# Extra products for TensorE in the last body and the tail of a cross-attention and mixture-of-experts kernel

## The reference

```python
def block(x, ctx):
    h = layernorm(x)
    q = rms_norm(h @ q_w.T + q_b, norm_q_w)
    k_img, v_img = rms_norm(ctx[:, :257] @ k_img_w.T + k_img_b, norm_k_img_w), ctx[:, :257] @ v_img_w.T + v_img_b
    k, v = rms_norm(ctx[:, 257:] @ k_w.T + k_b, norm_k_w), ctx[:, 257:] @ v_w.T + v_b
    x = x + (attention(q, k_img, v_img) + attention(q, k, v)) @ o_w.T + o_b
    h = layernorm(x)
    gate = top2(softmax(h @ Wg + bg))            # 8 experts
    for e in range(8):
        y = gelu(h @ W1[e] + b1[e]); y = gelu(y @ W2[e] + b2[e]); y = y @ W3[e] + b3[e]
        x = x + gate[:, e] * y
    return x
```

## Time and profile before

| | before |
|---|---|
| median of 3 runs | 842.35 us (840.61 to 843.66) |
| time of the profiled execution | 840.39 us |
| its span, first to last instruction | 838.5 us |
| PE busy | 759.5 us, 91% of the span |
| DVE, ACT, POOL busy | 599.0, 491.5, 240.5 us |
| mean granted clock of PE | 0.958 of full speed |

### The profile page before, as it was taken

One profiled execution on the slowest core, in us unless ns is written; L12 is line 12 of the kernel. 1 busy time (PEld: TensorE's weight loads), 2 busy tenths in 40 slices (PEclk: granted clock), 3 DMA queues, 4 the chain that ended last, 5 costly groups with the idle time before them and its releaser, 6 DMA issues.

```text
span 838.5 us, 17282 instructions
## 1 busy us (share of the span) xinstructions
PE 759.5 (91%) x5906; PEld 658.8 (79%) x5906; DVE 599.0 (71%) x1269; ACT 491.5 (59%) x1136; POOL 240.5 (29%) x302
## 2 busy tenths in 40 slices
PE   4889899989898989775499999999999999999994
PEld 3657677767676767454499999999999999999993
DVE  6767878787878796765576868576676858676664
ACT  4377777777777767585154645555554555554443
POOL 3523334343434242214300504032140505032010
PEclk9989999999999999776599999999999999999998
DMA  9720102011111110232755665748575665748561
GB/s 315 281 81 6 58 4 68 27 51 44 35 61 35 60 32 17 87 121 84 258 194 189 246 223 222 247 154 291 212 249 198 245 230 217 253 163 288 197 218 64
DMA packets 29205, 126.28 MB, mean 151 GB/s; under 512 B 4204, under 2 KB 4220, under 8 KB 19424
## 3 DMA queue, kind: packets, MB, share of 16 engines
q1 hardware_dynamic: 23696, 109.80, 37.1%
q0 software_dynamic: 5456, 15.81, 5.3%
HBM read 108.42 MB, written 18.74 MB: 152 GB/s over the span
## 4 chain that ended last, share of the span: by engine, by line
PE 70%; DVE 11%; ACT 10%; issue 5%; DMA 2%; POOL 1%; SPq 0%; ACTq 0%; DVEq 0%; POOLq 0%
PE tiles L1174 7%; PE tiles L1176 6%; PE tiles L1175 6%; PE scores L1463 4%; PE scores L1461 4%; PE ptb L1289 4%; PE scores L1462 4%; PE pvb L1176 3%; PE pvb L1175 3%; PE ptb L1175 3%; PE pvb L1174 3%; PE ptb L1174 3%; PE ptb L1176 3%; PE scores L1279 2%; PE pvb L1312 2%
## 5 line engine op out<-in xcount | busy, mean ns | idle before, releaser
L918 DVE TENSOR_TENSOR w<-scr,w 128x2048 fp32r<-128x2048 f32 x75 | 170.8, 2289 | 59.4 <-ACT w L682 59.4
L682 ACT ACTIVATE w<-scr 128x2048 fp32r<-128x2048 f32 x76 | 144.8, 1908 | 54.9 <-PE scores L1463 54.9
L512 POOL DMA_INDIRECT out_dram<-scr,tok x17 | 18.0, 1059 | 301.7 <-DVE scr L1153 299.3
L664 ACT ACTIVATE scr<-scr,rsum 112x257 f32<-112x257 f32 x128 | 66.4, 519 | 61.7 <-DVE rsum L902 61.7
L1174 PE MATMUL tiles<-c,w 128*128 128x258 f32 (+2 forms) x272 | 80.4, 296 | 4.7 <-DVE c L1127 2.6
L1174 PE MATMUL tiles<-w 128*128 128x256 f32 (+1 forms) x288 | 82.9, 288 | 0.6
L1175 PE MATMUL tiles<-w 128*128 128x256 f32 (+1 forms) x288 | 81.2, 282 | 0.0
L1176 PE MATMUL tiles<-w 128*128 128x256 f32 (+1 forms) x288 | 81.2, 282 | 0.0
L1141 DVE CAST w<-scr 128x256 fp32r<-128x256 f32 (+1 forms) x144 | 42.0, 292 | 54.6 <-ACT scr L772 54.6
L1289 PE MATMUL ptb<-ident,scr 112*128 112x112 f32 x384 | 63.9, 277 | 18.0 <-ACT scr L672 16.4
L1175 PE MATMUL tiles<-c,w 128*128 128x258 f32 (+2 forms) x272 | 77.8, 286 | 0.0
(11 more groups left out here) (221 smaller groups left out, 2302.2 us busy)
## 6 DMA issues: line engine op xcount, KB each, us to landing
scr<-in_dram SPq DMA_DIRECT2D x76, 1024.0 KB, 4.9
scr<-in_dram SPq DMA_DIRECT2D x8, 750.0 KB, 5.1
scr<-slots_d SPq DMA_DIRECT2D x10, 528.0 KB, 5.4
scr<-in_dram SPq DMA_DIRECT2D x10, 512.0 KB, 8.2
slots_d<-rows SPq DMA_DIRECT2D x8, 528.0 KB, 11.6
xn<-in_dram SPq DMA_DIRECT2D x9, 256.0 KB
xb<-in_dram SPq DMA_DIRECT2D x8, 224.0 KB, 2.7
xr<-in_dram SPq DMA_DIRECT2D x8, 224.0 KB, 2.6
```

Of the source, the lines that this page charges most:

```text
L664: act.activation(probs[0:L, s, 0:IMG], probs[0:L, s, 0:IMG], ACT.Copy, scale=rsum[0:L, g, s, 0:1]).then_inc(S["normal_img"], 1)
L682: act.activation(EH[slot], raw[slot], ACT.Copy).then_inc(S["eh_done"], 1)
L918: dve.tensor_tensor(EL[slot], raw[slot], EH[slot].bitcast(F32), ALU.subtract).then_inc(S["el_done"], 1)
```

## The change

PE gets 89 extra products. Each multiplies 128 columns with 512 columns of `wH(WV)`, weights that lie in SBUF and that nothing overwrites until the first expert's activations are written; the result goes into that one of the two `tiles` banks that has nothing pending, and nothing reads it. Their places are the ends of slots, after the fill: two in each slot 1 to 15 of body LAST (30 products, bank 1), then 2, 2, 4, 11, 2 and 8 in slots 0, 1, 2, 6, 12 and 15 of body DONE (29, bank 0), 24 between the count of tokens and the wait for `slots_done`, and 6 behind the first `turn`. Two waits guard the banks: one for the copy of the last values out of bank 1 (ACT L639), ahead of the first pair, and one for `take_o` of sequence 6, at the start of DONE's. No other engine's stream changes.

```diff
+BUSY_AT = {LAST: {h: 2 for h in range(1, 16)}, DONE: {0: 2, 1: 2, 2: 4, 6: 11, 12: 2, 15: 8}}
...
+            def keep_busy(bank, n):
+
+                spare = wH(WV)
+                for _ in range(n):
+                    pe.matmul(tiles[:, bank, :], spare[:, 0:P], spare[:, 0:512], start=True, stop=True)
...
                     for name, lo, hi in FILL[h]:
                         if has(name, b) and not (fixed(b, DONE) and hi < NC):
                             stage(name, lo, hi, b, p)
+                    if fixed(b, LAST) and h == 1:
+                        bank, cnt = tile_use("o", DONE)
+                        pe.wait_ge(tile_free[bank], cnt)
+                    if fixed(b, DONE) and h == 0:
+                        taken(pe, "o", LAST)
+                    if b in BUSY_AT and h in BUSY_AT[b]:
+                        keep_busy(tile_use("o", DONE if fixed(b, LAST) else LAST)[0], BUSY_AT[b][h])
...
             pe.matmul(ptb[:, 0:E], ones[0:L, :], sofar[0:L, :], start=True, stop=True).then_inc(S["count_ready"], 1)
...
+            keep_busy(tile_use("o", LAST)[0], 24)
             pe.wait_ge(S["slots_done"], 1)
...
             turn(0, BLOCK)
+            keep_busy(tile_use("o", LAST)[0], 6)
```

## The result

The change takes 836.93 us in the median of 11 runs (834.62 to 839.66), the kernel before 841.6 us beside it (840.37 to 843.66). The ratio is 0.9948, 95% interval 0.9935 to 0.9961: faster by 0.5%, or 4.4 us by the ratio (4.7 between the medians). The forecast was -2.8 us, with a range of 835.2 to 844.0.

A forecast was written before the change was run, and what follows sets the result against it. PE was taken to bound most of the kernel, neither full nor fast at about 335 to 419 us. LAST +0.5 and the tail -3.3 gave -2.8 us, a median of 839.5 us, range 835.2 to 844.0.

The forecast's parts named there:

- The tail: After sequence 7's take_o: full clock shortens turn by 1.1 us and the experts' first 24 products by 2.3; -3.3 us with risk.
- What the change can give in LAST: Body LAST to DONE slot 0: terms +0.86, +1.0, +0.35 and -1.4 sum to +0.8 us, taken as +0.5.
- The fall at 348.0: LAST slots 0 and 1: one pair is too little, clock still falls; slots 2 to 4 stay at half, costing 0.86 us.
- Slots 10 to 12: Body LAST: even odds that the clock holds, gaining 2.0 less 1.0 us, or falls, losing 1.7; mean +0.35.
- The price of a pair: Six on-path pairs in LAST and DONE slot 0: 0.5 us each at full clock, 3.0 in all; 5.2 at half.
- the forecast's list: PE work on the path at half clock in LAST and DONE slot 0; full clock would save 7.0 us together.
- the best case of -4.0: Body LAST with the clock at full: 7.0 us gained less 3.0 for the six on-path pairs.
- Between the last output product and the turn: 387 to 406 us: DVE and POOL set the end, so fast clock gives nothing and products fitting the gaps are free.
- Risk of the 24: Products ahead of the first turn: half at half clock they take 8.0 of 7.97 us; 0 to 0.7 late, 0.1 charged.
- the first rival: Clock holds nearly throughout LAST: -4.0 - 3.3 = -7.3 us, so 835.0; chance 0.20.
- The rival in which the pairs are paid at half: LAST slots 3 to 11 and DONE 0: clock not held, 5.2 us paid, total +2.5, so 844.9; chance 0.15.
- The tail's gain: Rival that it is missing: half clock at turn or the 24 late; tail 0, LAST +0.5, 842.9; chance 0.15.

The follow-up runs named there:

- tail_only: The change without the 30 extra products of body LAST: 838.91 us against 842.0 before, ratio 0.9964.
- change_again: The change itself, unaltered, timed again beside the kernel before: 838.07 us against 840.84, ratio 0.9954.
- last_only: The change with only the 30 products of body LAST, none in DONE or around the first turn: 840.33 us against 842.0 before, ratio 0.9989.
- twelve: The change with 12 instead of 24 products ahead of the first turn: 838.65 us against 842.98 before, ratio 0.9951.
- no_small: The change without the 11, 2 and 8 products in slots 6, 12 and 15 of DONE: 837.63 us against 842.98 before, ratio 0.9943.
- off_path: The change without the pairs in LAST slots 3, 4, 5, 10, 11 and DONE slot 0: 836.98 us against 842.98 before, ratio 0.9936.
- at_waits: The change without its six on-path pairs, with 8, 6 and 4 products in LAST slots 1, 9 and 13: 833.4 us against 842.0 before, ratio 0.9899.
- four_per_slot: The change with four products instead of two in each slot of LAST: 840.64 us against 842.98 before, ratio 0.9981.
- at_waits_again: The kernel of at_waits, unaltered, timed again beside the change: 832.8 us against 840.84 before, ratio 0.99.

## Why the prediction was right, point by point

**The forecast of the time was right, its division was not.** The tail is worth -3.1 us by the stretches and -3.0 by `tail_only`, where the forecast had -3.3. That leaves about -1.6 of the change's -4.7 for body LAST, where the forecast had +0.5 (by the ratios, -1.4). So the part with the wrong sign is the last sum of "What the change can give in LAST". Against the stretch before, its four terms and what came, from the table above:

| | forecast | first profile | `change_again` |
|---|---|---|---|
| up to slot 4 | +0.86 | -0.81 | +1.18 |
| slots 4 to 8 | +1.0 | -0.44 | +0.55 |
| slots 8 to 12 | +0.35 | -0.73 | -0.73 |
| from there to the last output quarter | -1.4 | -1.41 | -1.41 |

That the total still lay in the range is in part the width of the range, 835.2 to 844.0, which holds "no change" as well. By the forecast's own sign (it is wrong if LAST grows or shrinks by over 2 us) the first profile, with -3.39, spoke against it, and the second, with -0.41, did not.

**The fall at 348.0.** The forecast had slots 2 to 4 at half throughout, on the ground that one pair in slots 0 and 1 is too little. A fall came in all five profiled executions with two per slot; in `change_again` it cost what was forecast or more. In the first profile the clock was back before the rank products, and slot 3's pair took 0.64 us and not 0.86. So the first two terms vary from one execution to the next, and the forecast was near their bad end.

**Slots 10 to 12.** Given even odds and +0.35 us. In all five profiled executions with pairs of two in these slots (the change twice, `last_only`, `twelve`, `no_small`) they keep the clock: by the timeline the scores of slot 12 start 7.75 to 7.77 us after those of slot 8 in each of them, against 8.61 before. That is the term that was wrong: the good one of the two cases, put at -1.0, came each time, and measured -0.73. `off_path`, where the pairs are missing, is the execution in which it fell there.

**The price of a pair.** Six on the path at 0.5 us were to cost 3.0. From start to start the six fill 0.64, 0.46, 0.47, 0.57, 0.63 and 0.46 us: 3.2. But that is what they fill and not what they cost. In `at_waits`, where they are gone and the clock is full, the stretches are shorter by 0.43 us for the two of slots 4 and 5, by 0.19 for those of slots 10 and 11, and by 0.48 for that of DONE; with at most 0.64 for slot 3 it is about 1.7. What was wrong is not the size of a pair but that all of it lies on the path: with the pairs gone and the clock full, PE waits for ACT in slots 6, 11 and 12 (0.30, 0.34 and 0.32 us). In `four_per_slot`, where those waits are used up, the second pairs of slots 3, 4 and 5 cost 0.47 and 0.91 us, all that they fill.

**What a full clock gives.** For the same reason the 7.0 us of the forecast's list were too many. `at_waits`, which has the clock at full from slot 1 on and no pair on the path, gains 5.30: 1.62, 0.87, 0.92 and 1.89 in the four stretches, where the list has 2.0, 1.1, 2.0 and 1.9. The two errors, in cost and in gain, largely cancel, so the best case of -4.0 is close to the -3.86 of `last_only` for a wrong reason.

**The pages on the clock and the gap.** The Trainium skill ("TensorE: Matmul & The Clock Gate", "Back-to-back issue gap") gives 131 ns for a 512-column product in a sustained stream; here it is 0.23 us from one to the next in every run of them at full clock. The Trainium skill (same page, "Why this matters for your kernels") blames idle gaps between bursts for a clock that falls in mid-kernel. In `off_path` PE is busy for 10.01 of 10.10 us at half clock and has no wait above 1.96 us in the whole body, so idle gaps alone do not explain this case.

**Between the last output product and the turn.** Forecast free and, behind take_o, useless at any clock. Shown by the 20.81 and 20.75 us at clocks of 0.57 and 0.92, and by `no_small`. Even the logits are read directly behind the table constants, as said.

**Risk of the 24.** Forecast 0 to 0.7 us late. They were 0.93 us early in the first profile and 0.98 in `tail_only`. In `change_again` and `four_per_slot` they took 7.96 and 7.95 us and just met the turn, and in `at_waits_again` they took 8.44 and the turn came 21.02 us after the output product, about 0.3 late. The forecast's 0.1 for this risk is fair. The rest of its -3.3 was 0.2 too large: the stretch from the turn to the experts gave 0.91 us and not 1.1, the first 24 products 2.19 and not 2.3.

**The rivals.** The clock held nearly throughout LAST in the first profile (39.15 us, -3.4), as the first rival had it but for slots 2 and 3, and the median lies between it and the forecast. The rival in which the pairs are paid at half did not come, though `change_again` shows its piece in slots 3 and 4. The tail's gain was not missing in any run that kept the 24 at 512 columns.

## What to carry to other kernels

A clock lost in a thin stage can be bought back with products that nothing reads: with 512 columns they did it here, with 8 they did not. They belong ahead of a wait. Eight, six and four products inside three waits did more than a pair in every slot, and a pair outside a wait cost up to half a microsecond. Before adding them, list for each slot whether PE's next instruction waits, and ask which engine ends last once PE is fast: the time that a product fills is not yet the time that it costs. Look at the stage behind the thin one as well, since here two thirds of the change's gain came from a dense stage that began at half clock. And take several profiles of one kernel before giving a stage a size, since this one came out at 39.15 and at 42.13 us.

## What the runs showed of the hardware that was not expected

**The same program finds its clock differently from one execution to the next.** With nothing changed in the kernel, the LAST stretch was 39.15 us in one profile and 42.13 in another. In the first the clock was full when LAST began and then fell for about 3 us; in the second it was at half when LAST began, came back, and then fell for about 10. The start of LAST itself, ahead of which no kernel differs, lies between 342.36 and 346.29 us in the thirteen profiles, so part of every spread above is made before the place that the change touches. The version with more work inside the waits took 36.97 to 37.27 us in three.

**One wait near the end can cost the same again.** The `last_only` execution of 844.16 us was 1.3 us ahead of before at the experts' 25th product, and 3.4 us behind at the end. Its last `turn` waited 1.73 us for rows from DRAM (0.46 before), and the clock fell:

```profile
822.21 1.12 PE L1437 MATMUL scores<-ident,scr 128*128 128x128 f32 x4 [1.73 <-DMA scr<-slots_d]
```

From the 25th product to that turn it was 2.03 us more than before, the turn took 0.46 more, and the chain behind it shows twelve products at up to 0.43 us, which are 0.23 at full clock: 2.3 more. `tail_only` has a smaller case of it, with a wait of 0.86 us, a turn of 1.07 instead of 0.66, and products at half behind it. This end is common to all the kernels here and no run changed it. From the 25th product to the end it is 426.71 us in this execution and 421.60 to 423.78 in the other twelve, so part of the spread of the times comes from there; what sets it was not tried.
